# A two-layer hybrid model on one core: another order of the pieces on every engine, and other places of the spare products

## What is computed

```python
x = x + delta_attention(_layernorm(x))   # scan over 128 steps, 4 sequences, 16 heads of 8, clipped updates
x = x + moe_ffn0(_layernorm(x))          # swiglu, top 2 of 8 experts
x = x + palette_attention(_layernorm(x)) # top 15 keys, gather, small MLP, bilinear palette
x = x + moe_ffn0(_layernorm(x))
x = x + linear_attention(_layernorm(x))  # causal, elu + 1 features
x = x + moe_ffn1(_layernorm(x))          # relu squared, top 2 of 8 experts
x = x + decay_attention(_layernorm(x))
x = x + moe_ffn1(_layernorm(x))
```

## Time and profile before

| | us |
|---|---|
| median of 3 runs | 1407.27 |
| lowest and highest | 1399.64, 1412.8 |
| span of the profiled execution | 1464.6 |

### The profile page before, as it was taken

How to read it: one execution, slowest core, us unless ns; L and a number is a source line. 1 busy time by engine, 2 the same in 40 slices (tenths; PEclk the granted TensorE clock), 3 DMA queues, 4 the chain that set the end, 5 groups by cost and what they waited for, 6 DMA issues and landing times.

```text
span 1464.6 us, 47170 instructions
## 1 busy us (share of the span) xinstructions
PE 1274.9 (87%) x18561; PEld 836.0 (57%) x18561; DVE 1034.3 (71%) x4437; ACT 817.4 (56%) x2193; POOL 909.4 (62%) x1320
## 2 busy tenths in 40 slices
PE   7877778898989898998989899999998889898886
PEld 3333545555646665666656575656566565666654
DVE  4768787788758768787767878787777855564442
ACT  3232353556566566667565656475663737566754
POOL 5345767677857576676766676667746546665431
PEclk8677778999979899899979998899989979999998
DMA  6000000101010000000010000000001010101000
GB/s 167 2 1 13 27 18 17 32 8 29 8 29 8 21 14 17 17 17 23 8 29 6 15 21 14 20 9 23 12 11 28 9 29 10 30 17 30 4 3 7
DMA packets 27256, 29.34 MB, mean 20 GB/s; under 512 B 12145, under 2 KB 22290, under 8 KB 27026
## 3 DMA queue, kind: packets, MB, share of 16 engines
q0 software_dynamic: 8336, 16.73, 4.6%
q1 hardware_dynamic: 18690, 9.51, 2.4%
HBM read 24.90 MB, written 2.29 MB: 19 GB/s over the span
## 4 chain that ended last, share of the span: by engine, by line
PE 41%; POOL 13%; issue 11%; DVE 11%; ACT 6%; another core or an unknown queue 1%; DMA 0%; POOLq 0%; DVEq 0%; ACTq 0%
PE ps L703 3%; PE ps L759 3%; POOL sb L1866 3%; PE ps L536 2%; PE ps L924 2%; PE ps L826 2%; PE ps L605 2%; PE ps L616 1%; PE ps L805 1%; PE ps L746 1%; PE ps L915 1%; DVE ps L1036 1%; PE ps L783 1%; PE ps L829 1%; PE ps L591 1%
## 5 line engine op out<-in xcount | busy, mean ns | idle before, releaser
L1866 POOL DMA_INDIRECT sb<-table,sb x240 | 241.5, 1006 | 82.5 <-issue 50.0
L1036 DVE TENSOR_TENSOR_SCAN ps<-ps,sb 128x47 f32<-128x47 f32 (+3 forms) x1024 | 270.8, 264 | 30.3 <-ACT sb L1439 1.5
L1028 DVE TENSOR_TENSOR ps<-sb,ps 128x24 f32<-128x24 f32 (+3 forms) x1024 | 193.3, 189 | 14.7
L536 PE MATMUL ps<-sb 128*128 128x512 bf16 x585 | 184.6, 427 | 10.9 <-ACT sb L1651 2.8
L1726 POOL TENSOR_TENSOR sb<-sb 128x1 f32<-128x1 f32 x128 | 72.9, 572 | 160.6 <-DVE sb L971 158.8
L605 PE MATMUL ps<-sb 32*32 32x32 f32 x2032 | 70.3, 209 | 42.8 <-DVE sb L1008 33.8
L605 PEld LDWEIGHTS ps<-sb 32*32 32x32 f32 x2032 | 41.4, 109 | 113.3 <-DVE sb L1008 66.8
L616 PEld LDWEIGHTS ps<-sb 32*32 32x32 f32 x2032 | 41.5, 108 | 99.5 <-DVE sb L1044 60.6
L1363 ACT ACTIVATE sb<-ps 128x128 f32<-128x128 f32 x128 | 35.1, 276 | 103.6 <-PE ps L559 96.4
L536 PEld LDWEIGHTS ps<-sb 128*128 128x128 bf16 x585 | 56.0, 107 | 64.7 <-issue 20.4
L977 DVE TENSOR_TENSOR sb<-ps,sb 128x128 f32<-128x128 f32 x112 | 32.2, 288 | 83.5 <-PE ps L887 29.5
(11 more groups left out here) (308 smaller groups left out, 3609.4 us busy)
## 6 DMA issues: line engine op xcount, KB each, us to landing
sb<-table,sb POOLq DMA_INDIRECT x240
sb<-in_cs SPq DMA_DIRECT2D x16, 128.0 KB
table<-sb SPq DMA_DIRECT2D x17, 64.0 KB, 1.5
sb<-dscr SPq DMA_DIRECT2D x64, 2.0 KB
out<-sb SPq DMA_DIRECT2D x16, 64.0 KB
sb<-in_x SPq DMA_DIRECT2D x3, 256.0 KB, 5.8
sb<-in_wex SPq DMA_DIRECT2D x1, 512.0 KB, 3.9
sb<-in_rvx SPq DMA_DIRECT2D x1, 512.0 KB, 4.2
```

The source lines that it names most:

```text
L536: e.matmul(b[:, 0:512], onesb[:, :], onesb[:, :].unsqueeze(1).to_broadcast([128, 4, 128]), start=True, stop=True)
L1028: e.tensor_tensor(at(psP, p + ROW - 3 - 2 * m, [ROW, 3], [2, m], [1, 2]), AC[:, row(n, k), :, HIST - 2 * m:HIST].rearrange("p r (a b) -> p ...
L1036: e.tensor_tensor_scan(at(psD, 16 + k + COMB * skip, [COMB, 3 * ROW - skip]), at(psP, p + skip, [1, 3 * ROW - skip]), Q[:, i % 32, skip:3 ...
L1866: e.indirect_dma_start(GA[:, k, :], None, table[0:128 * i + 128, :] if i else table0, bass.IndirectOffsetOnAxis(u[:, k:k + 1], 0)).then_in ...
```

## The change

The strings of `ORDER` for all five engines and the string `FILL` are others. Each string has the same letters equally often; no instruction of a stage is changed. One line of TensorE's string and one of `FILL`, before and after:

```diff
 ORDER = {
     "PE":
-        "sfffsggffssgzzgssfssgsfsssszsgsssfzsssszssgssszssgsfsszsgoszoosoossssfzfgssozossosasasasgsssaassasasasasgsssp"
...
+        "ssfffggffssgzzgssfssgsfsssszsgsssfzsssszssgssszssgsfsszsgozossoossszfsfgszoossoosasasasgsssaassasasasasgsssp"
...
 FILL = (
-    "0919090620400000000250300200200100000100100001001000000100000005000010200200000700009010000010200000000000000202000"
...
+    "019199071040000000025030026120010000220014002100103000110000403000110200000000000901100003320010104303000220"
```

More of the change, by code:

```diff
@@ L116 @@
[L116 to L120, removed]
@@ new lines @@
+    "POOL":
+        "zzffffggfggzggfffggggffgggggffggggoofgooooozooggfapffppppgggpoggohooooogoohafhhghhghhhhhphfhhhfppppfopoggoho"
+        "gfoooooagmhfhmghghhhhhmhhffgphhhpopphgopooooooofpgagghhghhhhmmhbhfphmhghghhppgpgfhpfloohllllooollloooopcaggf"
+        "gghhhdhhhhgghhhdhhdmmddghfmbffhgopgoggppoofoolpohlololglpalllpggchghhhhhghehdhhhmmhhhhdmdddbpfgooffpopoopoop"
+        "looggllpallfglllhgcgghhhmhhmhhehdmhhbpgfhhddfpddpoofghpohooloollologlllplgpagchhhfghehdhhhmghmhhddmdbfdghpgf"
+        "fhgoohphpooopopgooolpfllallllglghhhchmmgfhhggmhhedfhbphhhfhdhdddoohgpoppolooopgollgolllplagflhgghchhmghghhfh"
+        "mhhdehmhgbhhhpddddppoogopgoplooooopllfallflllggchhghhmhmhehdmgfbhhhhdpdhhpddhoppopoohooogoolllpfallglgllffgg"
+        "ghchhgghhmmedmhhhfbhphhddhdpdohpohgoooohlopoolplllfplallffggcgghghhghedhhghhfhhmmdmdddghghhbopoghhoofooooopp"
+        "lppfpfllllggalllgggcmmemdhgghhhhhhdghddhdhbohpohhhhoopppopoooploallllglllcmmhhedmhhhhhhhhhhdhddbdhhpoopppopo"
+        "olpoolllololllachhhhhhmmedhhmhhddhddbphhhhpppppbllllllllhhhhclhhllhllmllmlehdhmhhhhddhdcdhbldelmmlldlldmlldd"
+        "cbedllllllldldddceddddde",
@@ new lines @@
+    "940000000000004300012330710110000000000000053000101000000000300000010000001005221000000000010000402003003000"
+    "000000000000000042020000002006000021302104034300020000300200000400300000000002000000000000000000000000000000"
+    "000000000000000000000103034001010100000001000100333000006000000001000010100005000000003042010000100000009000"
+    "000000113100000020000000100200500000000000001000010020000003006000000010020222000200000023250500000100300000"
+    "000024000003010000000080400000000010000002012000200020000800000000006000000000300000000001400100100000100100"
@@ new lines @@
+    "000003000330030000000000000000000000200350000000001300901072020000000000000000000006060000000000000050020200"
+    "000000200020000000008050020024500000000000021000320000000401005000001000010000000000000000001000020000100000"
+    "400000030003001000003002000000000000000000000010010000200001120000000200000000040003030600000004100003400000"
+    "000041000002000000000003000000002100030100024020104001200000000000000020010000000000353004053011935100000000"
+    "000200000000000000000000000100400000010007000002010000100000000000000000000000000000000000000040004310000000"
@@ new lines @@
+    "011001003202000570143030000004010000830000000000000000000000000000000100000000100000000000000002000000000000"
+    "000200000200000000000003000120001100000100000000000200000004001004000000000500030030000000006030003200000000"
+    "000001000000000000100007201000000000000000090000000001000000003000000000003000000061100000215530000303020015"
+    "000040000040020300000001100004100010000100400000001000000000001430000000000000000000000000000010000100000184"
+    "030820000003000200001100000000000000000000001200000000000000000001022003000500110009000020001200010000500300"
```

179 lines of the change are left out of this document (79 added, 100 removed).

## The result

The changed kernel takes 1418.58 us (median of 5 runs, 1410.05 to 1419.78) against 1407.27 for the kernel before (5 runs); the ratio is 1.0077, with a 95% interval of 1.0044 to 1.0109. It is slower, by less than the 1% named as the border. It lies outside the forecast's range of 1372 to 1400, and outside 1367 to 1413 too.

The account below looks back on a forecast made before the run. No engine alone was the bound; TensorE was fullest, its idle time and lower clock winnable. Terms -1.3 + 4.1 - 3.1 - 8.3 - 10 = -18.6 us on 1464.6, scaled to 1389 us; forecast 1372 to 1400, 8-in-10 range 1367 to 1413.

Parts of the forecast that it names:

- The base: Whole kernel: profiled span 1464.6 us scaled to the runs' median 1407.27, giving 1389.4 us after the predicted saving.
- term 3: VectorE stalling on the port shared with GpSimd: 40 us in all, half avoided by the new order, -3.1 us.
- Changes of tile shape: TensorE's order: 1263 shape changes become 1250, at 0.10 us each, -1.3 us.
- Spare products: TensorE issues 667 instead of 585, 17.7 us added, mostly within waits: +4.1 us, ends 0 and +17.7.
- Port stalls: VectorE's L1116, L1238 and others held up beside GpSimd: half of 40 us avoided, -3.1 us, ends 0 and -10.
- Waits between engines: TensorE's and VectorE's existing waits shrink on balance under the new order: -8.3 us, ends +5 and -30.
- SyncE's queue: First tile's relation transfers now stand behind the table store, L1214 needs them: nothing, or up to +3 us once.
- The clock: TensorE: spare products at more long waits recover part of 269 us at 1.2 GHz: -10 us, ends 0 and -30.
- The signs: If right: L536 x667, TensorE idle under 175 us, clock 0.92, L605's waits for L1008 under 30, L1116 near 280 ns.
- No change: waits only move: Waits shift between L605, L616 and the norm chain without gain: 1410 us, in all 1394 to 1420; chance 0.28.
- The slow rival: TensorE's added spare products are not covered by waits and delay products behind them: 1424 us, up to 1440; chance 0.14.

Follow-up runs that it names:

- before: The kernel before, unchanged: apparently the profile read for the forecast, spanning 1464.6 us, like those of slow chips.
- before_look_2: The kernel before, unchanged, profiled on a quick chip: 1405.0 us.
- after_again: The changed kernel itself, timed and profiled on a slow chip against the kernel before: 1526.83 us, ratio 1.0388.

## Why the prediction was wrong

The forecast was 1389 us, -1.3%; the time is +0.8%. By its steps:

- **The base.** The step "scaled to that, 1407.27 x (1446.0 / 1464.6)" took the 57 us between profile and runs for a common factor. They were another kind of chip, on which TensorE stands still (30.9 us of "issue" waits against 5.6), with what hung on it. This changed the forecast's sum by less than 1 us (1407.27 - 18.6 is 1388.7), but every term was read from a trace of a kind of chip on which the runs shown had not been made. The 4.46 us at 214.14 is no such stall, though its row says "issue": L605 starts 0.05 us after VectorE's transpose L1008 has ended, and on a quick chip the same product waits for it as long:

```profile
217.05 0.33 PE L605 MATMUL ps<-sb 32*32 32x32 f32 x8 [3.90 <-DVE sb L1008]
```

So term 3 was right to count it as VectorE being late.
- **Changes of tile shape (-1.3).** No run tells this apart; it is far below what the runs resolve.
- **Spare products (+4.1).** The count of 667 is right. On the order for which they were placed they cost 0 (1392.0 against 1392.1 us without gathers), the first of the two ends. But the same products on the old order cost 20 us without gathers, more than the 17.7 us that was given as the most they could. How is not shown; that a late product also delays the exchange behind it would fit L616's 18.3 us in the table, but that is argued.
- **Port stalls (-3.1).** The size of what went away was about right; no gain in time came of it. L1116 and L1238, kernel before on a quick chip:

```profile
L1116 DVE SCALAR_TENSOR_TENSOR sb<-sb 128x8 f32<-128x8 f32 x64 | 22.8, 357 | 0.9
...
L1238 DVE TENSOR_SCALAR sb<-sb 128x32 f32<-128x32 f32 x16 | 11.0, 687 | 0.6
```

and in the changed kernel, answering to the earlier trace rows:

```profile
L1116 DVE SCALAR_TENSOR_TENSOR sb<-sb 128x8 f32<-128x8 f32 x64 | 16.3, 257 | 1.1 <-ACT sb L1639 0.2
...
L1238 DVE TENSOR_SCALAR sb<-sb 128x32 f32<-128x32 f32 x16 | 8.4, 526 | 0.6
```

The means fall from 357 to 257 and from 687 to 526 ns, and VectorE's busy time falls by 22 us, about the half of 40 us that was assumed. In all profiles with gathers VectorE is busy for 1029.9 to 1034.3 us with the old order and spare products, and 1010.8 to 1012.0 us in the changed kernel; without gathers 1007.8 and 1000.7, so two thirds of the difference hang on the gathers. The Trainium skill's rule of the lock (SBUF — State Buffer, section on the two separate sides) says that whoever comes second is blocked. The prediction's reading of it, that moving pieces only chooses who loses, would have had the means stay; they did not. Yet the end came no earlier: in its place VectorE waits for TensorE, at L1051 alone 10.3 us more.
- **Waits between engines (-8.3).** This is the step that failed, and in sign. In place of -8.3 us the order costs 10 us without gathers (1.0072 and 1.0079 in two pairs), beyond even the worse end of +5. The step looked only at waits that the old order had and asked whether they shrink. That selects gains: the waits that a new order makes are not in the old trace, as the end "+5" admitted. L616's wait for L1044 went from 13.0 to 20.5 us and L1051's for L616 from 46.2 to 56.5.
- **SyncE's queue (0 to +3).** Right with 0. The first tile's relations now follow the table store at once, and L1214 starts at 184.77 us, not after 189; changed kernel:

```profile
179.62 0.32 SPq L2028 DMA_DIRECT2D table<-sb  x1
180.03 2.46 SPq L2045 DMA_DIRECT2D sb<-dscr  x4
184.77 0.75 DVE L1214 SCALAR_TENSOR_TENSOR sb<-ps,sb 128x512 f32<-128x512 f32 x1
```

- **The clock (-10).** This step failed too: it measured nothing where 10 us were forecast. The median clock is 0.929 and 0.931 on the two quick chips before and 0.929 after; on chip 10, a slow one, it is 0.907 before and 0.893 after. That spare products stand at more of the old order's long waits did not raise it. The price was of the right size: 0.5 x 0.41 = 0.205 us for each microsecond at 1.2 GHz, where the two runs with and without spare products give 0.19 net of the products' own cost, and so somewhat more without it. That spare products hold up the clock, and that this pays, is shown by the kernel without any: 3.5% slower at 0.823 in place of 0.909, on a slow chip.
- **The signs.** Four of the signs of being right came true: L536 x667, L1116's mean near 280 ns (257), TensorE's idle time under 175 us (159) and a clock of 0.92 or more. But the last two hold for the kernel before on a quick chip as well (158 us, 0.929), so they told of the chip and not of the change. L605's waits for L1008 under 30 us did not come true (38.9).
- **The rivals.** "No change: waits only move" (1394 to 1420) holds the time and names what happened on quick chips: the time that left L1116 came back in waits of L616 and L1051. The slow rival named the spare products; on their own order they are not the cause. The case that cost most, gathers during which TensorE stands still on slow chips, was not among the rivals.

What is shown: the gathers cause the stalls on slow chips (replacing them saves 90 us there against 22 us on a quick chip, and leaves 6.1 of some 30 us of "issue" waits), and GpSimd's string sets how many. What is shown by pairs of runs without gathers only: that the order costs 0.7% besides, a good half of it by GpSimd's string. Which pieces do it is open; the windows put it between 500 and 1150 us. On quick chips with the gathers in place, order and spare products were not taken apart.

Open too is what differs between the chips, whether a gather's bytes or descriptors are in the way, and what of TensorE they hold up. "Instruction feed" in the expectations is a guess. The transfers of instructions are in the trace, and they take the same share on a slow and on a quick chip (`before` and `before_look_2` alike: packets, MB, share of 16 engines); in the stretch of `after_again` shown above none lies between 443.25 and 447.60 us:

```profile
q8 instruction: 149, 2.44, 0.7%
q14 instruction: 81, 0.66, 0.2%
```

None of the kernels that compute the full result was faster than the kernel before.

## What to carry to other kernels

If the profiled execution is some per cent longer than the timed runs, don't scale: find out first which waits make the difference, above all those for nothing that the trace shows, since the timed chip may not have them. A new order can't be judged by the waits of the old one, because it makes its own; and time won on an engine in an exchange of two is only worth what the other can follow. Spare products belong to the order for which they were placed: the new ones cost 15 to 20 us on the old order and nothing on the new one. A mean clock read from one profile is that of one run; compare medians of several before a difference of 0.006 is given a cause.

## What the runs showed of the hardware

- One program took 1404 and 1468 us on different chips, steadily on each. On the slow chips TensorE stood still during GpSimd's gathers for nothing that the trace shows: in streams of tiny products the starts came in steps of some 0.7 us (444.55, 445.29, 446.04, 446.75). Without gathers both kinds took 1381 to 1382 us.
- 585 spare products, 126 us of issue, are worth 52 us on a slow chip: the clock of the profiled run is 0.909 with them and 0.823 without.
- TensorE was still granted 1.00 from 444 to 446 us while it stood still, and 0.50 from 446.75 us when the stream went on; the stall cost a second time through the clock.
- A gather of 64 bytes a row in place of 512 left the time as it was within 0.3% on a quick chip.
- An instruction of VectorE on 8 columns (L1116, 64 times) took 357 ns in the mean with the old order and 257 ns with the new one, on chips of the same kind.
